# Second attention: the scores of a tile's four head groups issued together into four banks, and new orders

## The chip, the cores and the metric

One core of a Trainium2 chip runs the program in one launch. The metric is the device time in microseconds (us) on that core. The kernel before took 264.71 us, the median of three runs that lie between 264.69 and 265.05 us. TensorE is called PE here, as in the profile, VectorE DVE, ScalarE ACT and GpSimd POOL; PEld is PE's weight load.

## The reference

Two batches of 512 tokens with 128 channels pass a Flamingo-like block of two layers, all in float32:

```
layer 0: cross attention, 8 heads of 64 channels, keys = 512 tokens + 77 context rows, then out @ Wout
         gated add:  x1 = x + tanh(gx0) * attention(layernorm(x), layernorm(ctx))
         feed-forward with weights and activations rounded to few levels:
         512 hidden channels, a convolution of three taps along the tokens, silu;  x2 = x1 + tanh(gf0) * ...
layer 1: cross attention, 16 heads of 8 channels over the 77 context rows, rotary positions:
         scores = q @ k^T / sqrt(8);  p = softmax(scores);  out = p @ v;  y = out @ Wo^T + bo
         x3 = x2 + tanh(gx1) * y
         mixture of 8 experts (the best 2 by a router) plus a shared one, 64 hidden channels each
         out = x3 + tanh(gf1) * ...
```

The change is to the scores of the attention of layer 1, and to the order of everything.

## The kernel before

All data stay on the chip once loaded. The 512 tokens of a batch are four tiles of 128 rows. The work is cut into items, a kind with its numbers: for a batch b `x0` is the normalised input turned, `k`, `q`, `v` the projections of the first attention, `u` one head and tile of it (64 in all), `w` its product with the values, `o` its output projection, `n` the normalisation behind it, `f1` to `f4` the feed-forward (turning the input, first matrix with convolution by chunk, quantising by tile, second matrix by tile). For the second attention `a1` turns two tiles of the input, `a2` makes their queries, `a3` keys and values, `a4` is one tile with 8 of its 16 heads (16 items: 2 batches, 4 tiles, 2 halves), `a6` the product with the values and the output for two tiles. `m1` to `m4` are the experts.

An item has stages: F (front, on PE), B (back, on PE), A1 and A2 on ACT, D0 to D3 on DVE, P1 and P2 on POOL, and Ca or Cd, a copy by ACT or by DVE. For an `a4` item the chain is

- F: two matmuls at line 672, each with 32 rows of the array (four heads of 8 channels, kept apart by zeros in `KBD`), 308 columns, into two neighbouring banks of PSUM
- D1: the negated maximum of each head (`mx`, line 1152, DVE)
- A1: eight exponentials into `S` (line 910, ACT)
- B: five transposes back into the same two banks (line 518, PE)
- C: the copy of these into `PT` (line 787 on ACT or 789 on DVE); only then are the two banks free.

PSUM has eight banks. An item whose F says `F4` takes bank 4, and 5 as well if it is wide, as `a4`, `u`, `k`, `m2` and `m4` are; its F waits until what held these banks before is done with them (`banks_left`). For `a4` that is the copy C.

The order of the work is written out by hand in the table `PLAN`, one word a stage: each engine walks its own stages in the order of the table and waits for semaphores, and nothing overtakes. A word like `a4:B+20@2` puts 20 transposes of the identity into bank 2 ahead of the stage, which keep PE at work where it would wait. There are 85 such fillers. Semaphore `front_done` counts the F stages in PE's order, and DVE and ACT wait for an item's number in it (`NTH`).

## Time and profile before

| | us |
|---|---|
| median of the runs | 264.71 (264.69 to 265.05) |
| the profiled execution | 264.35 |
| its span, first to last instruction | 262.4 |
| PE busy | 254.0 (97%) |
| DVE busy | 217.1 (83%) |
| ACT busy | 192.2 (73%) |
| POOL busy | 31.1 (12%) |

Busy is the time in which an engine had an instruction under way. Matmuls are pipelined and their ends are modelled, so PE at 97% is not PE at its peak, and the fillers count as busy. Transfers matter only at the start: 0.52 MB is written and 4.99 MB read from memory in the whole span.

### The profile page before, as it was taken

Reading aid. Unit: us, or ns where it says so; the run is one execution under the profiler, and the core shown is the slowest. Engines: PE = TensorE matmul, PEld = TensorE weight load, DVE = VectorE, ACT = ScalarE, POOL = GpSimd, SP = SyncE. Lnnn points to the kernel's source line nnn. Section 1 sums busy time; section 2 is a strip of 40 time slices with the busy share of each in tenths; the row PEclk is TensorE's granted clock in tenths of the full one; section 3 lists DMA queues with packets and bytes.
Section 4 is the critical chain, followed back from the end, with each engine's and each line's share of the span. In section 5 each row is a group of like instructions: output and inputs, shape, how many; then the busy total and the mean of one; then the engine's idle time right before and its main releaser. Section 6 shows DMA issues by size and latency. Waiting matters only on the chain.

```text
span 262.4 us, 5607 instructions
## 1 busy us (share of the span) xinstructions
PE 254.0 (97%) x1869; PEld 189.2 (72%) x1869; DVE 217.1 (83%) x534; ACT 192.2 (73%) x463; POOL 31.1 (12%) x53
## 2 busy tenths in 40 slices
...
DMA packets 8848, 10.70 MB, mean 41 GB/s; under 512 B 1115, under 2 KB 5877, under 8 KB 8821
## 3 DMA queue, kind: packets, MB, share of 16 engines
...
q10 hardware_dynamic: 1029, 0.65, 0.8%
...
HBM read 4.99 MB, written 0.52 MB: 21 GB/s over the span
## 4 chain that ended last, share of the span: by engine, by line
PE 70%; DVE 18%; ACT 5%; issue 5%; POOL 1%; DVEq 0%; ACTq 0%; POOLq 0%
PE slot L518 19%; PE slot L608 13%; PE slot L589 6%; PE slot L590 6%; PE slot L564 3%; PE slot L615 3%; DVE mx L1152 3%; PE slot L570 2%; PE slot L761 2%; PE slot L755 2%; DVE RB L1157 2%; ACT S L910 2%; PE slot L706 2%; PE slot L749 2%; PE slot L579 2%
## 5 line engine op out<-in xcount | busy, mean ns | idle before, releaser
L1046 DVE TENSOR_REDUCE nm<-slot 128x1 f32<-128x589 f32 x64 | 47.6, 766 | 9.7 <-PE slot L590 9.3
L838 ACT ACTIVATE PR<-slot,nm 128x589 f32<-128x589 f32 x64 | 47.7, 749 | 9.3 <-DVE nm L1046 8.8
L518 PE MATMUL slot<-K,PR 128*128 128x128 f32 (+1 forms) x320 | 44.3, 276 | 0.2
L589 PE MATMUL slot<-KH,Q 128*128 128x296 f32 (+1 forms) x128 | 42.1, 345 | 0.2
L518 PEld LDWEIGHTS slot<-K,PR 128*128 128x128 f32 (+1 forms) x320 | 36.1, 142 | 8.1 <-ACT PR L838 5.0
L608 PE MATMUL slot<-PT,V 128*64 128x256 f32 (+1 forms) x320 | 38.1, 384 | 0.7 <-ACT PT L773 0.7
L773 ACT ACTIVATE PT<-slot 128x640 f32<-128x640 f32 x47 | 32.2, 705 | 8.3 <-PE slot L518 7.3
L590 PE MATMUL slot<-KL,Q 128*128 128x296 f32 (+1 forms) x128 | 36.1, 299 | 0.0
L910 ACT ACTIVATE S<-slot,mx 128x77 f32<-128x77 f32 x128 | 29.2, 365 | 6.3 <-DVE mx L1152 5.6
L608 PEld LDWEIGHTS slot<-PT,V 128*64 128x64 f32 (+1 forms) x320 | 22.1, 137 | 12.3 <-issue 3.5
L589 PEld LDWEIGHTS slot<-KH,Q 128*128 128x128 f32 x128 | 24.2, 189 | 3.6 <-issue 1.4
L590 PEld LDWEIGHTS slot<-KL,Q 128*128 128x128 f32 x128 | 24.3, 190 | 1.7 <-issue 1.4
L468 POOL TENSOR_TENSOR vex<-vex,mhalf 128x2 f32<-128x2 f32 (+1 forms) x15 | 10.8, 720 | 83.7 <-DVE vex L986 83.7
L484 POOL COPY REC<-rec 128x256 f32<-128x256 f32 x16 | 6.8, 422 | 111.4 <-DVE rec L1022 85.9
L775 DVE COPY PT<-slot 128x640 f32<-128x640 f32 x17 | 13.8, 815 | 1.8 <-PE slot L518 1.8
L1040 DVE TENSOR_TENSOR KL<-slot,KH 64x590 fp32r<-64x590 f32 x16 | 12.2, 765 | 2.7 <-ACT KH L871 2.3
L1152 DVE TENSOR_REDUCE mx<-slot 128x8 f32<-128x616 f32 x16 | 12.6, 794 | 0.3 <-PE slot L672 0.3
L838 ACT ACTIVATION_READ_ACCUMULATOR PR<-slot,nm 128x1 f32 x64 | 12.6, 197 | 0.0
L518 PE MATMUL slot<-K,S 128*128 128x128 f32 x80 | 11.7, 279 | 0.6 <-ACT S L910 0.6
L1033 DVE SCALAR_TENSOR_TENSOR Q<-slot,Q 64x512 fp32r<-64x512 f32 x16 | 11.0, 689 | 1.3 <-ACT Q L863 0.9
L871 ACT ACTIVATE KH<-slot 64x590 fp32r<-64x590 f32 x16 | 10.5, 654 | 2.3 <-PE slot L581 2.1
L518 PEld LDWEIGHTS slot<-K,S 128*128 128x128 f32 x80 | 8.8, 140 | 3.9 <-ACT S L910 3.5
...
## 6 DMA issues: line engine op xcount, KB each, us to landing
...
```

The costliest lines, as they stand in the source:

```text
L518: return pe.transpose(dst, src, ident[0:p, 0:p])
L589: pe.matmul(W[:, K0 + lo:K0 + hi], q, KH[:, g % 4, lo:hi], start=True, stop=False)
L590: mm = pe.matmul(W[:, K0 + lo:K0 + hi], q, KL[:, g % 4, lo:hi], start=False, stop=True)
L608: mm = pe.matmul(W[e * DH0:(e + 1) * DH0, 0:N], V[0:r, c, h * DH0:(h + 1) * DH0], PT[0:r, s, c, e, :], start=(c == 0), stop=(c == 4))
L773: engine.activation(dst, src, ACT.Copy).then_inc(pt_copied["ACT"], 1)
L775: engine.tensor_copy(dst, src).then_inc(pt_copied["DVE"], 1)
L838: act.activation(PR[:, s, :], W[:, K0:K0 + KEYS0], ACT.Exp, bias=nm0[:, s:s + 1], accum_out=sum0[:, b, p * 2 + f, t, e:e + 1]).then_inc(pr ...
L910: act.activation(S1[:, s, j * C:(j + 1) * C], W[:, at:at + C], ACT.Exp, bias=mx1[:, s, j:j + 1]).then_inc(exp1_ready, 1)
L1033: dve.scalar_tensor_tensor(out=Q[o, s, e, :], in0=W[r, 0:S], scalar=float(DH0) ** 0.5, in1=Q[r, s, e, :].bitcast(F32), op0=ALU.mult, op1=A ...
L1040: dve.tensor_tensor(KL[r, s, :], W[r, K0:K0 + KEVEN], KH[r, s, :].bitcast(F32), ALU.subtract).then_inc(k_ready, 1)
L1046: dve.tensor_reduce(nm0[:, s:s + 1], W[:, K0:K0 + KEYS0], AX.X, ALU.max, negate=True).then_inc(max_ready, 1)
L1152: dve.tensor_reduce(mx, w, AX.X, ALU.max, negate=True).then_inc(max1_ready, 1)
```

## The change

PE no longer has an F stage for the first half of a tile's `a4` pair. The F of the second half issues all four matmuls, on the four groups of 32 rows, into the four banks of both halves, and it waits for the former holders of all four. A new semaphore `scores1_ready` is counted up by the second and by the fourth matmul; DVE waits for it in place of `front_done`. D1, A1, B and C stay as they are, an item each. `PLAN` is written anew. The fillers are 68 now, where there were 85. Who makes the copies changes too:

| copies by DVE | before | after |
|---|---|---|
| `u` | 17 | 12 |
| `f3` | 4 | 6 |
| `a4` | 2 | 2 |

Up to the last `w` of batch 1 (its F on PE, its D1 on DVE) the two programs have the same items, and so behind it, but for copies: behind it DVE has lost one `QB` copy (line 814) and kept two `PT` copies.

```
-x0:F6 x0:A1 k:F0 q:F6 k:A1 k:F2 k:D1 q:A1 v:F4 q:D1 v:F0 k:A1 v:Ca k:D1 u:F6 u:F2 v:Ca u:F4 u:D1 u:D1 u:A1 u:A1 u:F0 u:D1
...
+x0:F2 x0:A1 k:F0 k:A1 k:D1 q:F6 k:F2 q:A1 q:D1 v:F4 v:F0 k:A1 k:D1 v:Ca v:Ca u:F6 u:F2 u:F4 u:D1 u:A1 u:F0 u:D1 u:B u:A1
...
-NTH = {x: n for n, x in enumerate(x for x, stage in ORDER["PE"] if stage == "F")}
+NTH = {x: n for n, x in enumerate(x for x, stage in ORDER["PE"] if stage == "F" and x[0] != "a4")}
...
+        scores1_ready = sem("scores1_ready")
...
                 if kind != "f1":
                     warm(item, "F")
+                if kind == "a4":
+                    if item[3] == 0:
+                        return
+                    for former in HAD[item[:3] + (0,)]:
+                        banks_left(former)
                 for former in HAD[item]:
                     banks_left(former)
...
                     _, b, t, h = item
                     pe.wait_ge(q1_ready, (b * QT + t) // TP + 1)
                     pe.wait_ge(kbd_ready, b + 1)
-                    for n in range(2):
-                        rows = slice((2 * h + n) * 32, (2 * h + n + 1) * 32)
-                        mm = pe.matmul(W[:, n * 512:n * 512 + G1 * C], Q1[rows, t * P:(t + 1) * P], KBD[rows, b],
+                    for g in range(G1):
+                        rows, scores = slice(g * 32, (g + 1) * 32), slot(("a4", b, t, g // 2))
+                        mm = pe.matmul(scores[:, g % 2 * 512:g % 2 * 512 + G1 * C], Q1[rows, t * P:(t + 1) * P], KBD[rows, b],
                                        start=True, stop=True)
+                        if g % 2:
+                            mm.then_inc(scores1_ready, 1)
+                    return
...
-                act.wait_ge(front_done, NTH[item] + 1)
+                if kind != "a4":
+                    act.wait_ge(front_done, NTH[item] + 1)
...
-                dve.wait_ge(front_done, NTH[item] + 1)
+                if kind == "a4":
+                    dve.wait_ge(scores1_ready, n)
+                else:
+                    dve.wait_ge(front_done, NTH[item] + 1)
...
                     if b == 1:
-                        dve.wait_ge(front_done, NTH["a4", 0, QT - 1, 1] + 1)
+                        dve.wait_ge(scores1_ready, 2 * QT)
```

The banks of the `a4` items of batch 1 are these, with what each must wait for. An item is written as tile and half.

| item | bank before, former holder | bank after, former holder |
|---|---|---|
| 0.0 | 2, `a4` of batch 0, tile 3 | 4, `a4` of batch 0, tile 3 |
| 0.1 | 0, `a2`, `a4` of batch 0 | 0, `a4` of batch 0 |
| 1.0 | 4, `a4` of batch 0, tile 3 | 4, item 0.0 |
| 1.1 | 2, item 0.0 | 2, `m1`, `a4` of batch 0 |
| 2.0 | 0, item 0.1 | 0, item 0.1 |
| 2.1 | 4, item 1.0 | 6, `a6`, `a2` |
| 3.0 | 6, `m1`, `a6` | 6, item 2.1 |
| 3.1 | 4, item 2.1 | 4, `m3`, item 1.0 |

What moves is seen on two engines in that same stretch. First ACT from the exponentials of tile 0 on: in these rows `S<-slot,mx` x8 is one A1 (x16 two in a row), `PT<-slot` a copy C, `LT<-slot` belongs to `a1` or `m1`, `SHT` and `lg` to `m3`, and `HM` and `slot<-slot` to `m2`. Before:

```order
L910 ACTIVATE S<-slot,mx 128x77 x16
L787 ACTIVATE PT<-slot 128x5x128
L910 ACTIVATE S<-slot,mx 128x77 x16
L787 ACTIVATE PT<-slot 128x5x128
L913 ACTIVATE LT<-slot 128x256
L910 ACTIVATE S<-slot,mx 128x77 x16
L918 ACTIVATE SHT<-slot 128x128
L923 ACTIVATE lg<-lg 128x16
L910 ACTIVATE S<-slot,mx 128x77 x8
L787 ACTIVATE PT<-slot 128x5x128 x2
```

After:

```order
L920 ACTIVATE S<-slot,mx 128x77 x8
L910 ACTIVATE LT<-slot 128x256
L923 ACTIVATE LT<-slot 128x256
L920 ACTIVATE S<-slot,mx 128x77 x8
L796 ACTIVATE PT<-slot 128x5x128
L920 ACTIVATE S<-slot,mx 128x77 x16
L796 ACTIVATE PT<-slot 128x5x128 x2
L920 ACTIVATE S<-slot,mx 128x77 x8
L928 ACTIVATE SHT<-slot 128x128
L933 ACTIVATE lg<-lg 128x16
L920 ACTIVATE S<-slot,mx 128x77 x8
L796 ACTIVATE PT<-slot 128x5x128 x2
```

Two rows `LT<-slot` stand now between the two A1 of tile 0, and the copies of a tile come behind both its A1 or, for tile 2, behind `SHT`, `lg` and the second A1. Before, a copy stood between most of the A1.

Then DVE, from the reciprocal of the second `a6` of batch 0 (`RB<-slot`) on: `mx<-slot` is D1 of an `a4` item, `RC` and `Q<-RC` are `a2`, `X<-slot,tg,X` with the three rows behind it is D2 of `a6`, `PT<-slot` a copy, `XN` D3 of `a6`, and `lg<-slot` starts `m3`. Before:

```order
L1157 RECIPROCAL RB<-slot 128x256
L1158 TENSOR_TENSOR A1T<-slot,RB 128x256
L1152 TENSOR_REDUCE mx<-slot 128x8
L789 COPY PT<-slot 128x5x128
L1238 SCALAR_TENSOR_TENSOR X<-slot,tg,X 128x256
L980 BN_STATS bnx<-X 128x6 x2
L981 BN_AGGR mvx<-bnx 128x2 x2
L986 TENSOR_SCALAR vex<-mvx 128x2
L1152 TENSOR_REDUCE mx<-slot 128x8
L789 COPY PT<-slot 128x5x128
L1152 TENSOR_REDUCE mx<-slot 128x8
L989 TENSOR_SCALAR XN<-X,mvx,vex 128x128 x2
L1163 COPY lg<-slot 128x16
```

After:

```order
L1170 RECIPROCAL RB<-slot 128x256
L1171 TENSOR_TENSOR A1T<-slot,RB 128x256
L1165 TENSOR_REDUCE mx<-slot 128x8 x2
L1155 SCALAR_TENSOR_TENSOR RC<-slot,COL,K 128x256 x2
L1158 TENSOR_TENSOR Q<-RC 128x256
L1251 SCALAR_TENSOR_TENSOR X<-slot,tg,X 128x256
L990 BN_STATS bnx<-X 128x6 x2
L991 BN_AGGR mvx<-bnx 128x2 x2
L996 TENSOR_SCALAR vex<-mvx 128x2
L1165 TENSOR_REDUCE mx<-slot 128x8 x2
L798 COPY PT<-slot 128x5x128
L1176 COPY lg<-slot 128x16
```

The two `mx` of a tile are neighbours now (`x2`). Before, single `mx` rows alternate with other work.

## Rows read from the trace of the kernel before

**Rows 1.** The page, section 1: busy time, share of span, instructions

```profile
PE 254.0 (97%) x1869; PEld 189.2 (72%) x1869; DVE 217.1 (83%) x534; ACT 192.2 (73%) x463; POOL 31.1 (12%) x53
```

**Rows 2.** Windows: PE, PEld, DVE, ACT, POOL busy (count), PEclk, DMA share, GB/s

```profile
0.00:165.90 165.90, 162.66 (x1165) 126.57 (x1166) 135.33 (x309) 126.29 (x256) 15.09 (x34) 1.00 0.22 60
165.90:204.40 38.50, 36.74 (x297) 26.31 (x295) 35.25 (x87) 30.73 (x93) 4.20 (x6) 1.00 0.01 2
204.40:224.50 20.10, 19.28 (x190) 12.45 (x187) 18.92 (x51) 16.87 (x66) 2.21 (x3) 1.00 0.01 2
224.50:241.90 17.40, 17.16 (x117) 10.45 (x115) 15.61 (x57) 9.33 (x27) 5.82 (x8) 1.00 0.02 6
241.90:262.40 20.50, 18.12 (x108) 13.41 (x108) 11.98 (x34) 9.03 (x22) 3.73 (x4) 1.00 0.08 23
```

**Rows 3.** Windows, line 672 alone: PE busy, PEld busy, PEclk; one item, then two

```profile
210.73:211.44 0.71, 0.71 (x4) 0.30 (x4) 1.00 0.00 0
203.04:203.90 0.86, 0.80 (x8) 0.31 (x8) 1.00 0.00 0
215.33:216.32 0.99, 0.96 (x8) 0.47 (x8) 1.00 0.00 0
```

**Rows 4.** Timeline of DVE, 208 to 224: start, us, what, [idle <-releaser]

```profile
208.01 0.87 DVE L1142 SCALAR_TENSOR_TENSOR RC<-slot,COL,K 128x256 f32<-128x256 f32 x2
...
209.25 0.59 DVE L989 TENSOR_SCALAR XN<-X,mvx,vex 128x128 f32<-128x128 f32 x2
209.77 1.75 DVE L1157 RECIPROCAL RB<-slot 128x256 f32<-128x256 f32 x1
...
211.89 0.79 DVE L1152 TENSOR_REDUCE mx<-slot 128x8 f32<-128x616 f32 x1
212.60 0.81 DVE L789 COPY PT<-slot 128x640 f32<-128x640 f32 x1
213.33 0.47 DVE L1238 SCALAR_TENSOR_TENSOR X<-slot,tg,X 128x256 f32<-128x256 f32 x1
...
214.72 0.80 DVE L1152 TENSOR_REDUCE mx<-slot 128x8 f32<-128x616 f32 x1
...
217.41 0.17 DVE L1163 COPY lg<-slot 128x16 f32<-128x16 f32 x1
...
221.16 1.76 DVE L1157 RECIPROCAL RB<-slot 128x256 f32<-128x256 f32 x1 [0.21 <-DVE cwt L1230]
...
223.68 0.80 DVE L1152 TENSOR_REDUCE mx<-slot 128x8 f32<-128x616 f32 x1 [0.30 <-PE slot L672]
```

**Rows 5.** Timeline of ACT, 200 to 219

```profile
200.19 1.83 ACT L910 ACTIVATE S<-slot,mx 128x77 f32<-128x77 f32 x8 [0.62 <-DVE mx L1152]
...
205.36 3.55 ACT L910 ACTIVATE S<-slot,mx 128x77 f32<-128x77 f32 x16 [1.51 <-DVE mx L1152]
209.96 0.70 ACT L787 ACTIVATE PT<-slot 128x640 f32<-128x640 f32 x1 [1.05 <-PE slot L518]
...
215.02 0.44 ACT L913 ACTIVATE LT<-slot 128x256 f32<-128x256 f32 x1
...
218.93 0.39 ACT L918 ACTIVATE SHT<-slot 128x128 f32<-128x128 f32 x1
```

**Rows 6.** Timeline of PE, 206 to 223

```profile
206.43 1.50 PE L684 MATMUL slot<-PT,V 128*32 128x256 f32 x24 [0.23 <-DVE X L1238]
...
222.85 0.79 PE L672 MATMUL slot<-KBD,Q 32*128 32x308 f32 x4
```

**Rows 7.** Timeline of DVE, 174 to 190

```profile
174.76 0.69 DVE L1091 TENSOR_TENSOR XL<-slot,XH 128x512 fp32r<-128x512 f32 x1 [0.40 <-PE slot L672]
...
189.85 0.43 DVE L814 TENSOR_SCALAR QB<-W 128x512 bf16<-128x512 f32 x1
```

**Rows 8.** Timeline of DVE near 238

```profile
238.57 1.03 DVE L1169 TENSOR_TENSOR lg<-lg,top 128x16 f32<-128x16 f32 x1
```

**Rows 9.** Timeline of POOL near 238

```profile
238.52 1.04 POOL L506 TENSOR_TENSOR HM<-HM,cwt 128x512 f32<-128x512 f32 x1
```

**Rows 10.** The page, section 4: the chain that ended last, by engine

```profile
PE 70%; DVE 18%; ACT 5%; issue 5%; POOL 1%; DVEq 0%; ACTq 0%; POOLq 0%
```

More of the change, by code:

```diff
@@ new lines @@
+u:D1 u:B u:D1 u:A1 u:Ca u:A1 s:D2 u:B u:Ca u:F6 u:Cd u:B u:F4 u:D1 u:F2 u:Ca u:A1 u:D1 v:F0 u:A1 u:D1 s:F1 u:B v:Ca
+u:B u:A1 u:Ca q:F0 u:Ca s:D1 q:A1 w:D0 u:B k:F6 u:F4 q:D1 k:A1 k:D1 w:P1 u:Ca w:F1 u:D1 w:A1 u:F6 w:D1 u:F2 u:D1 u:F0
+u:A1 u:B u:D1 u:A1 u:A1 u:D1 u:B u:Cd u:B u:A1 w:D0 u:Cd u:F4 w:P1 u:D1 u:B u:F6 u:Ca q:F3 u:D1 w:F2 u:A1 x0:D2 w:D0
+u:A1 u:B q:A1 u:Ca u:B q:D1 w:A1 u:F0 u:Ca w:D1 u:D1 w:P1 u:F4 u:Ca u:A1 u:D1 u:F2 u:A1 u:D1 u:A1 a3:F6 u:B u:B u:B
+a3:D1 u:Ca u:Ca u:F0 k:F4 g:F6 u:D1 u:Ca u:F2 u:D1 k:A1 w:F7 k:D1 u:A1 w:D0 x0:P2 u:A1 u:B g:D1 u:B u:Ca x0:D3 w:P1 u:F4
@@ new lines @@
+u:Ca u:D1 w:A1 u:A1 q:F6 w:D1 u:F0 q:A1 u:F2 u:B w:F7 u:D1 u:A1 u:Cd u:F4 w:A1 q:D1 w:D0 u:D1 u:A1 u:B w:D1 u:D1 u:Ca
+u:F6 u:B u:A1 u:D1 u:F0 u:A1 u:B u:Cd x0:F2 u:Ca u:D1 u:B u:A1 w:P1 a3:P1 a3:F4 x0:A1 u:Ca u:B k:F2 u:Ca a3:D1 k:A1 u:F6
+u:F0 w:D0 u:D1 k:D1 w:F5 u:A1 u:D1 u:B u:A1 q:F2 w:A1 u:B u:Ca w:D1 u:F4 w:P1 u:F6 u:D1 u:D1 q:A1 u:Cd q:D1 w:F3 u:A1
+u:A1 u:B u:B w:A1 u:Ca u:F0 u:Ca u:F4 w:D0 u:D1 w:D1 u:A1 u:D1 w:P1 w:F6 u:B u:F2 u:A1 w:A1 w:D1 u:D1 u:B u:Ca u:Cd
+o:F6 u:F0 o:D1 u:A1 u:B u:Ca u:D1 u:F6 u:A1 u:D1 w:D0 u:F4 q:F3 u:B u:D1 u:A1 u:Ca a3:P1 q:A1 w:P1 u:B q:D1 u:Cd w:F2
@@ new lines @@
+u:A1 u:B+2@0 u:F0 u:F6 u:Ca w:A1 o:F3 u:D1 u:F4 u:A1 u:D1 w:D1 u:B o:D1 n:P2 u:A1 o:F3 u:D1 o:D1 n:D3 u:B u:Ca u:A1 w:D0
+v:F0 k:F2 u:Ca u:B v:Ca u:F6 v:F0 k:A1 u:D1 u:Ca u:F4 k:D1 u:D1 u:A1 v:Ca u:A1 u:B u:Cd u:F2 k:F0 u:D1 u:A1 u:B o:F6
+k:A1 u:B u:Cd k:D1 u:Ca v:F7 o:D1 u:F4 w:P1 v:Ca u:D1 u:F2 u:F6 u:D1 u:A1 w:D0 u:A1 w:F1 u:D1 u:A1 u:B u:B n:P2 w:A1
+u:Ca n:D3 u:B u:Ca u:F4 f1:F0 u:D1 q:F2 u:Ca f1:A1 f1:D1 u:F6 u:A1 w:D1 u:D1 q:A1 w:D0 u:B f2:F3 q:D1 u:Ca u:F0 f2:A1 u:D1
+w:P1 u:F4 u:A1 w:F2 u:D1 u:A1 f2:D1 u:B u:B u:A1 u:B w:A1 u:Ca f2:A2 w:D1 u:Cd f2:F6 f2:D2 w:P1 u:F2 f2:F7 u:Ca u:F0 u:D1
@@ new lines @@
+k:F4 f2:A1 u:A1 f2:D1 u:D1 f2:A1 k:A1 u:B f2:D1 k:D1 w:D0 u:A1 w:F6 u:B f2:A2 f2:F7 w:P1 u:Ca w:A1 u:Ca f2:A1 u:F2 u:F4 f2:D2
+w:D1 u:D1 u:F0 f2:A2 u:D1 u:A1 w:F6 u:A1 u:B f2:D1 f2:A2 w:A1 u:D1 f2:D2 f2:D2 u:B f3:F7 u:A1 u:Ca u:B u:Ca u:F2 u:F4 u:Ca
+w:D1 f3:D1 f3:A1 u:D1 f3:F6 q:F0 u:D1 f3:D1 u:A1 f3:F1 f3:D1 u:B u:A1 w:D0 f3:A1 u:Ca f3:Cd u:B u:Ca f3:Cd u:F6 f3:A1 q:A1 u:D1
+w:P1 u:F2 f4:F5 w:F4 f4:A1 q:D1 f4:B u:D1 f4:D2 u:A1 u:B w:A1 u:F0 u:A1 u:Ca w:D1 f4:F5 u:D1 f4:A1 f3:F4 u:B f3:D1 f3:Cd w:D0
@@ new lines @@
+u:A1 u:F6 f4:B u:Ca f3:A1 u:B f4:D2 u:F2 u:Ca w:P1 u:F4 w:F1 f4:F0 u:D1 u:A1 f3:Cd u:D1 u:A1 u:D1 u:B u:A1 u:Ca w:D0 f4:A1
+u:B u:B u:Cd w:A1 u:F6 f4:B u:F2 w:P1 w:D1 u:Ca f4:P2 f4:D2 w:F4 f4:F5 u:D1 u:A1 u:D1 u:B u:A1 w:A1 w:D1 u:Ca u:F0 f4:A1
+f4:D3 u:D1 u:B u:F6 o:F4 u:D1 u:Ca u:A1 u:A1 o:F2 o:D1 u:B f4:B w:D0 u:B w:P1 o:D1 f4:D2 n:P2 u:Ca u:Ca f4:P2 a1:F1 n:D3
+w:F5 f4:D3 a1:A1 w:A1 a2:F2+3@0 a1:F7 w:D1 o:F6 a2:D1 a4:F2 o:F5 o:D1 o:D1 a4:F0 n:P2 a1:A1 a4:D1 a2:F4 a4:D1 a4:A1 a4:A1 a4:B+17@5 n:D3 f1:F5
```

47 lines of the change are left out of this document (12 added, 35 removed).

## The prediction

> **What bounds the kernel now.** I read the page's busy shares first, then the windows by stage, then the timelines of the stretch that the change touches. The page says PE at 97% and DVE at 83% [rows 1], and the chain of waits is PE for 70% and DVE for 18% [rows 10]. That invites the thought that work taken off PE shortens the run. The windows by stage say where that holds and where it does not [rows 2]. Up to 165.9 us, the end of the first attention, DVE is busy 135.33 of 165.9 us and PE 162.66: PE is the limit. From 241.9 on DVE is busy 11.98 of 20.5 us and PE holds the end. Between the two lies all of the second attention, and there DVE is the busier engine than its mean suggests: 35.25 of 38.5, 18.92 of 20.1 and 15.61 of 17.4 us. The counts of PE in these windows contain nearly all of the 85 fillers, which are no work. So the middle, 76 us long, is paced by DVE walking its list without a pause. A change there pays by what it does to DVE's list and to DVE's waits. PE's work there is cover.
>
> The waits of DVE in that middle are few: 0.40 us at the feed-forward of batch 1 [rows 7], 0.21 and 0.30 us later on [rows 4]. The three windows leave 3.25 + 1.18 + 1.79 = 6.2 us in which DVE was not busy, over 195 instructions [rows 2]; of this 2.9 us are waits of 0.1 us and over, the rest is the step from one instruction to the next.
>
> **The change part by part.** The profiled execution took 264.35 us with a span of 262.4; the median of the runs is 264.71. My sum is a difference against the profiled execution, and I add it to the median.
>
> *Scores four at a time.* One item's two matmuls occupy PE 0.71 us. Where two items of different halves happened to meet, the four took 0.86 us together in one place and 0.99 in another [rows 3], so the four groups of rows already overlap here. Eight tiles at 0.86 are 6.9 us, against 12 items alone at 0.71 and two such pairs (0.86 and 0.99), 10.4 us. PE loses 3.5 us of work, and 17 fillers with it. What hides both is DVE's list, so they cost and bring nothing: 0 us. If DVE's waits were all caused by PE they could bring at most the 2.9 us named above.
>
> *The copy.* DVE has one `QB` copy less in the middle: 0.43 us off [rows 7]. All other DVE work of the middle is the same set of instructions.
>
> *The collision.* A subtraction on 16 columns took DVE 1.03 us at 238.57, while POOL began a product on 512 columns at 238.52 [rows 8, 9]; a row of that size takes 0.17 [rows 4]. In another order it need not meet. Bounds: -0.9 and 0; I take -0.9.
>
> *First stage and tail.* Both have the same items on PE as before, and PE is their limit. The five `PT` copies that go from DVE to ACT there lie beside PE's work. I take 0 for both, with 0.7 us either way for other gaps; without cover each copy would be 0.7 us on ACT [rows 5].
>
> *The new waits, batch 1.* This is the main term. A tile now needs four banks at once, and its PE instruction waits for the last of the former holders. By the table of banks tile 1 needs bank 4 from item 0.0, tile 2 bank 0 from item 0.1, and tile 3 bank 6 from item 2.1; a bank comes back only when the copy C is done. ACT's list puts that copy behind both A1 of the tile (tile 0 with two `LT` between, tile 2 with `SHT` and `lg`). So I follow one tile's first `mx` to the next tile's first `mx`, once through ACT and once through DVE's own list. Prices: `mx` 0.71 to the next instruction and 0.80 to its end, a hand-over between engines 0.07 (a copy ends at 210.66, the scores that waited for its bank start at 210.73 [rows 3, 5]), a further A1 3.55 - 1.83 = 1.72, an `LT` 0.44, a copy 0.70 [rows 5], scores to `mx` 222.85 to 223.68 = 0.83 [rows 4, 6]. On DVE: `a2` 1.24, an `XN` pair 0.52, D1 of `a6` 2.12, copy 0.73, D2 of `a6` 1.39, `m3` 3.75 less the `mx` in it and the wait of 0.21, 2.83 [rows 4].
>
> Tile 0 to 1: 0.87 until A1 starts, 1.72, two `LT` 0.88, 1.72, copy 0.70, 0.07, 0.83 = 6.8 us. DVE has `mx`, `XN`, `mx`, `XN`, D1 of `a6` to do, 0.71 + 0.52 + 0.71 + 0.52 + 2.12 = 4.6. It waits 2.2 us.
> Tile 1 to 2: 0.87 + 1.72 + 1.72 + 0.70 + 0.07 + 0.83 = 5.9. DVE has two `mx`, `a2`, D2 of `a6`: 1.42 + 1.24 + 1.39 = 4.1. It waits 1.9.
> Tile 2 to 3: ACT first copies item 1.0, so A1 starts at about 1.3, ends at 3.0, then `SHT` and `lg` behind DVE's `lg`, to 3.5, A1 to 5.2, two copies to 6.6, and 0.9: 7.5. DVE has two `mx`, a copy, `XN` and `m3`: 1.42 + 0.73 + 0.52 + 2.83 = 5.5. It waits 2.0.
> Together 6.1 us. Behind tile 3 DVE's list is the old work with 0.9 us of waits, where before 1.3 us stood from 204.4 on. Net: +5.7. The other end is 0: were each bank back in time, as before, where the same chain found other DVE work beside it.
>
> *The new waits, batch 0.* The same walk there: tile 1's scores wait for the copy of item 0.0, which ACT has behind `XH` (DVE waits 0.65), the first chunk of the feed-forward stands behind them on PE (0.75), tile 2's scores wait for the quantising of tile 1 of the feed-forward (0.3), and behind these on PE stand the first `f4` and the 48 records of an `a6`, two times 1.4 us [rows 6], which DVE's first `f4` needs (1.15), then 0.45 more; the first `a2` wait is 0.46. That is 3.8 us, against 1.2 now (the 0.40 of [rows 7] among it), +2.6. The other end is 0. These hand-overs are less certain than those of batch 1, since each hangs on the one ahead of it, and all but one are of the size of waits that exist now; I take a third, +0.9.
>
> Sum: 0 - 0.4 - 0.9 + 0 + 5.7 + 0.9 = +5.3 us. The tail of 20.5 us starts when DVE frees bank 0 for the third `m4` of batch 0, at the end of that list, and PE cannot work ahead of its order, so it moves as a whole. Forecast 264.7 + 5.3 = 270.0 us.
>
> The rows show two items overlapping at 0.86 us [rows 3]. The Trainium skill, "TensorEngine Tiling (Array Packing)", section "Restrictions and Gotchas", says that row tiling raises PSUM pressure, since different row tiles write to different banks, and its section "PSUM Bottleneck" says that after such a speedup the copy out of PSUM may become the limit. This trace agrees in kind: the copy, 0.70 us, is what gives a bank back. That speaks against the change in the way of my main term. By its headline alone, up to four times faster for 32 rows, one would book the PE saving; I do not, because DVE paces this stretch.
>
> **Rivals.**
> *A, PE's relief reaches the end (faster).* The order feeds DVE as well as now or better, and scores come earlier for both halves. For it: overlap is real [rows 3], and 0.30 us of DVE's wait is for line 672 [rows 4]. Against it: the walk above uses durations that repeat all through the timeline. It would give -0.4 for the copy, down to -0.9 for the collision and some of the 2.9 us of waits: -2 us, 262.7, at best -4.2, 260.5.
> *B, the waits only change places.* The new waits are about as long as those removed, because PE or ACT run ahead further than I see: -0.4 to +0.4, 264.7.
> *C, the clock falls.* PE would wait up to 3.8 us at a time between tiles 1 and 2 (5.9 less some 1.9 of work), with no filler there. The granted clock is 1.00 in every window [rows 2], that is 2.4 GHz, with fillers in all long waits. Should it drop to 1.2 GHz, 5 us of PE work would take 10, so 275. Against it: nothing in this trace shows it drop after a wait.
> *D, the four matmuls do not overlap.* A tile would cost 1.42 us, and as the scores are on the walked chain, eight times 1.42 - 0.86 = 0.56 more, 4.5 us: 274.5. [Rows 3] speak against it twice.
>
> **How the numbers follow.** My forecast 0.66, its own range 267 to 272.5 (batch 1 at 4 to 6.1, batch 0 at 0 to 2.6, gaps 0.7). A 0.20, B 0.08, C 0.04, D 0.02. This kernel's runs tell no change from one of 0.2%, 0.5 us. Faster: A and a part of B, 0.22. Same: the middle of B, 0.06. Slower 0.72. The range that leaves out no more than 0.2 goes from 262.8, inside A, to 272.8.
>
> **What would show it.** In the profile after: line 678 in eight groups of 8 records, about 0.86 us from the first to the next instruction. On DVE, waits of 1.5 us and more ahead of the first `mx` of tiles 1, 2 and 3 of batch 1, released by line 678, and on PE waits ahead of line 678 released by the copy at line 796. DVE busy falls by some 4 us over the run, the span grows. The third `m4` of batch 0 starts about 5 us later than 241.95, and from there to the end it is 20.5 us. I am wrong if the largest waits of DVE there stay under 0.7 us, if A1 of the second half starts without waiting for its predecessors on ACT, or if the first stage ends more than 1 us away from 165.9.

## The result and the profile after

The changed kernel takes 274.38 us (median of four runs, 273.29 to 274.79), the kernel before 264.88 beside it (264.69 to 265.61). The ratio is 1.0336, with an interval of 1.0308 to 1.0364: 9.5 us slower. The direction was forecast; the forecast was 270.0 with a range up to 272.8, so the size was not. The profiled execution took 274.61 us with a span of 272.7, 10.3 more than the span before.

From the page of the kernel after, the busy times and the row of the granted clock in 40 slices:

```profile
PE 252.9 (93%) x1852; PEld 191.5 (70%) x1852; DVE 213.9 (78%) x531; ACT 194.6 (71%) x466; POOL 31.2 (11%) x53
PEclk9999999999999999999999999978998989999999
```

PE, DVE and POOL are busy for about as long as before or less [rows 1], DVE for 3.2 us less; ACT is busy for 2.4 us more, still 71% of its span. So for DVE, which paced the middle before, the 10.3 us are waits. The clock row is new: before it was full in every slice.

The windows of four stretches of the kernel after, where the granted clock (the number behind the bracket of POOL) stood at half, that is 1.2 GHz, and one behind them:

```profile
176.50:179.90 3.40, 3.40 (x16) 2.38 (x17) 1.59 (x3) 0.71 (x2) 0.00 (x0) 0.50 0.00 0
183.35:186.80 3.45, 3.02 (x14) 3.02 (x15) 3.38 (x6) 3.45 (x13) 0.00 (x0) 0.51 0.02 5
203.80:207.20 3.40, 3.40 (x14) 3.28 (x15) 2.71 (x5) 3.40 (x15) 1.39 (x2) 0.50 0.02 5
217.50:220.90 3.40, 3.40 (x13) 2.94 (x13) 2.74 (x5) 2.64 (x13) 0.00 (x0) 0.50 0.01 2
224.00:242.00 18.00, 15.93 (x157) 10.01 (x156) 14.30 (x51) 12.23 (x45) 3.56 (x5) 1.00 0.00 1
```

Where the time went is seen best on DVE, cut at the same instructions in both kernels: from the first score reduction (`mx`) of batch 0 to the first of batch 1, on to the last of batch 1, and on to the end. Windows of DVE alone, first of the kernel before (start and end, length, busy and count, clock, DMA share, GB/s):

```profile
170.25:204.49 34.24, 31.90 (x77) 1.00 0.01 1
204.49:223.68 19.19, 18.02 (x49) 1.00 0.01 2
223.68:262.40 38.72, 28.40 (x91) 1.00 0.05 15
```

and of the kernel after:

```profile
170.82:210.54 39.72, 32.02 (x79) 0.87 0.00 1
210.54:232.22 21.68, 14.86 (x43) 0.92 0.01 2
232.22:272.70 40.48, 30.15 (x95) 0.99 0.05 14
```

Length less busy is what DVE did not work (the two orders share the busy time out differently over the stretches, so only its sum is compared):

| | before | after | difference | forecast |
|---|---|---|---|---|
| up to the first stretch | 170.25 | 170.82 | +0.57 | 0 |
| batch 0, not busy | 2.34 | 7.70 | +5.36 | +0.9 |
| batch 1, not busy | 1.17 | 6.82 | +5.65 | +5.7 |
| behind it, not busy | 10.32 | 10.33 | 0.0 | 0 |
| busy in all three | 78.33 | 77.03 | -1.30 | -0.4 - 0.9 |
| sum | | | +10.3 | +5.3 |

One line is off by far, and it is off by 4.5 of the 5.0 us by which the sum is off. The other half microsecond is the later start, and it can't be put down to the change: the first reduction starts between 170.25 and 171.75 us in runs that are like the kernel before up to there, and between 170.26 and 171.38 in those that are like the kernel after.

Batch 1, the timeline of DVE in the kernel after (start, us, engine and line, what, and in brackets the idle time ahead of it and its releaser):

```profile
210.54 0.80 DVE L1165 TENSOR_REDUCE mx<-slot 128x8 f32<-128x616 f32 x1
211.76 0.79 DVE L1165 TENSOR_REDUCE mx<-slot 128x8 f32<-128x616 f32 x1
217.43 1.50 DVE L1165 TENSOR_REDUCE mx<-slot 128x8 f32<-128x616 f32 x2 [1.98 <-PE slot L678]
223.30 1.51 DVE L1165 TENSOR_REDUCE mx<-slot 128x8 f32<-128x616 f32 x2 [0.65 <-PE slot L678]
231.50 1.51 DVE L1165 TENSOR_REDUCE mx<-slot 128x8 f32<-128x616 f32 x2 [2.62 <-PE slot L678]
```

From tile to tile that is 6.9, 5.9 and 8.2 us, where the walk gave 6.8, 5.9 and 7.5. (Between tiles 2 and 3 ACT waits 0.76 us for the transposes ahead of its two copies, which stand on PE behind the matmuls of `a6`; the walk left them out.) In the kernel before, the first reductions of tiles 0, 1 and 3 were these (tile 2's is in [rows 4]):

```profile
204.49 1.50 DVE L1152 TENSOR_REDUCE mx<-slot 128x8 f32<-128x616 f32 x2
207.29 0.80 DVE L1152 TENSOR_REDUCE mx<-slot 128x8 f32<-128x616 f32 x1
...
218.38 0.79 DVE L1152 TENSOR_REDUCE mx<-slot 128x8 f32<-128x616 f32 x1
```

2.8 us from tile 0 to tile 1, 3.7 from tile 2 to tile 3. How the chain runs between tiles 0 and 1 is seen on ACT:

```profile
211.38 1.83 ACT L920 ACTIVATE S<-slot,mx 128x77 f32<-128x77 f32 x8 [1.79 <-DVE mx L1165]
213.57 0.39 ACT L910 ACTIVATE LT<-slot 128x256 f32<-128x256 f32 x1 [0.36 <-PE slot L519]
213.85 0.38 ACT L923 ACTIVATE LT<-slot 128x256 f32<-128x256 f32 x1
214.11 1.83 ACT L920 ACTIVATE S<-slot,mx 128x77 f32<-128x77 f32 x8
215.77 0.77 ACT L796 ACTIVATE PT<-slot 128x640 f32<-128x640 f32 x1
```

and on PE, whose four matmuls wait for the last of these:

```profile
216.59 0.80 PE L678 MATMUL slot<-KBD,Q 32*128 32x308 f32 x8 [2.30 <-ACT PT L796]
```

The copy ends at 216.54, the scores start at 216.59, DVE's reduction at 217.43: each step as priced. A tile's four matmuls occupy PE 0.73 us to the next instruction, where the prediction took 0.86 from [rows 3].

Batch 0, DVE's waits of 0.4 us and more in the kernel after:

```profile
177.76 1.51 DVE L1165 TENSOR_REDUCE mx<-slot 128x8 f32<-128x616 f32 x2 [1.17 <-PE slot L678]
180.78 0.75 DVE L1110 SCALAR_TENSOR_TENSOR YC<-slot,cw,YC 128x511 f32<-128x511 f32 x1 [1.51 <-ACT YC L892]
189.71 0.69 DVE L1118 TENSOR_REDUCE aq<-slot 128x1 f32<-128x512 f32 x1 [0.42 <-PE slot L519]
194.01 0.80 DVE L1165 TENSOR_REDUCE mx<-slot 128x8 f32<-128x616 f32 x1 [0.51 <-DVE aq L1121]
197.83 0.35 DVE L1215 SCALAR_TENSOR_TENSOR X<-slot,aq,X 128x128 f32<-128x128 f32 x1 [1.12 <-PE slot L740]
207.89 0.48 DVE L1155 SCALAR_TENSOR_TENSOR RC<-slot,COL,K 128x256 f32<-128x256 f32 x1 [1.29 <-PE slot L670]
```

The walk had 0.65 and 0.75 for the first two and 1.15 for the fifth; the last, for the queries of `a2`, it had at under half a microsecond. The three that exceed it lie in or right behind the stretches at half clock. The tail moved as a whole: the third `m4` of batch 0 starts at

```profile
252.24 0.77 PE L519 MATMUL slot<-K,HM 128*128 128x128 f32 x5
```

and 20.5 us are left from there, as before.

### The profile page after: what moved, and what is told of

Its sections match the earlier page's. It is cut to its first block, busy times and chain, and to the rows that moved or that the text cites. A ratio compares the mean times of both kernels' runs of the same rounds, so it can differ in the third digit from the quotient of the medians.

```text
span 272.7 us, 5563 instructions
## 1 busy us (share of the span) xinstructions
PE 252.9 (93%) x1852; PEld 191.5 (70%) x1852; DVE 213.9 (78%) x531; ACT 194.6 (71%) x466; POOL 31.2 (11%) x53
## 4 chain that ended last, share of the span: by engine, by line
PE 73%; ACT 11%; DVE 10%; issue 5%; ACTq 0%; DVEq 0%
PE slot L519 23%; PE slot L614 12%; PE slot L595 5%; PE slot L596 5%; ACT S L920 5%; PE slot L570 3%; PE slot L770 2%; PE slot L764 2%; PE slot L678 2%; PE slot L621 2%; PE slot L576 2%; PE slot L715 2%; PE slot L758 2%; PE slot L585 2%; PE slot L670 1%
## 5 line engine op out<-in xcount | busy, mean ns | idle before, releaser
L595 PE MATMUL slot<-KH,Q 128*128 128x296 f32 (+1 forms) x128 | 41.5, 341 | 0.2
L782 ACT ACTIVATE PT<-slot 128x640 f32<-128x640 f32 x52 | 35.5, 704 | 7.8 <-PE slot L519 7.1
L519 PE MATMUL slot<-K,S 128*128 128x128 f32 x80 | 14.0, 323 | 3.4 <-ACT S L920 3.4
L519 PEld LDWEIGHTS slot<-K,S 128*128 128x128 f32 x80 | 11.2, 167 | 7.4 <-ACT S L920 5.8
L796 ACT ACTIVATE PT<-slot 128x640 f32<-128x640 f32 x14 | 10.0, 732 | 6.2 <-PE slot L519 6.1
L678 PE MATMUL slot<-KBD,Q 32*128 32x308 f32 x64 | 6.9, 505 | 7.8 <-ACT PT L796 6.6
```

The costliest lines, as they stand in the source:

```text
L519: return pe.transpose(dst, src, ident[0:p, 0:p])
L595: pe.matmul(W[:, K0 + lo:K0 + hi], q, KH[:, g % 4, lo:hi], start=True, stop=False)
L678: mm = pe.matmul(scores[:, g % 2 * 512:g % 2 * 512 + G1 * C], Q1[rows, t * P:(t + 1) * P], KBD[rows, b], start=True, stop=True)
L782: engine.activation(dst, src, ACT.Copy).then_inc(pt_copied["ACT"], 1)
```

## The experiments

Times are medians, with the kernel before beside them on the same chip; that one moved between 265.1 and 265.9 from one chip to the next, so the ratios are what is compared. Each edit is made on the kernel after or the kernel before, as said.

The first stage moves by one or two microseconds from run to run, so differences of that size are read from the profiled executions by stretch, in us: the start of the first score reduction of batch 0, from there to the first of batch 1, on to the last of batch 1, and on to the end.

| kernel | first reduction | batch 0 | batch 1 | behind it |
|---|---|---|---|---|
| before | 170.25 | 34.24 | 19.19 | 38.7 |
| before, no fillers (e4) | 170.03 | 35.84 | 19.19 | 38.7 |
| before, two tiles packed (e16) | 170.73 | 34.04 | 19.14 | 38.7 |
| before, three tiles packed (e5) | 170.82 | 34.07 | 20.59 | 38.7 |
| before, four tiles packed (e6) | 172.01 | 34.08 | 26.92 | 38.7 |
| before, more on DVE (e7) | 171.75 | 34.26 | 23.70 | 38.8 |
| before, copy moved (e9) | 170.46 | 34.25 | 19.24 | 38.7 |
| before, two copies moved (e12) | 170.31 | 34.26 | 21.03 | 38.7 |
| old then new (e10) | 170.82 | 36.55 | 27.62 | 40.5 |
| new then old (e11) | 170.51 | 41.34 | 18.37 | 38.7 |
| the same with fillers (e14) | 170.47 | 38.92 | 19.97 | 38.7 |
| after | 170.82 | 39.72 | 21.68 | 40.5 |
| after with fillers (e1) | 171.38 | 37.58 | 21.75 | 40.5 |
| after, scores two at a time (e2) | 172.92 | 38.95 | 21.90 | 40.6 |
| after, copies first (e3) | 170.29 | 38.51 | 20.55 | 40.5 |
| after, fillers and copies first (e13) | 170.26 | 37.59 | 21.00 | 40.5 |

### The kernel after with fillers at PE's waits (e1)

```
-a4:F2 a4:F6 a2:D1
+a4:F2 a4:F6+13@7 a2:D1
...
-f2:F0 f2:D2
+f2:F0+12@0 f2:D2
...
-a4:F4 a4:F2 a4:D1
+a4:F4 a4:F2+20@3 a4:D1
```

Nine stages have fillers ahead of them like these, 107 in all (the expectation counts 109).

> The kernel after, with 109 more fillers (transposes of the identity) written at PE's longest waits of the second attention, in banks that are free there; all else as after. In the kernel after the granted clock stood at half in four stretches of 3.41 us, and it was lower at no place of the kernel before. Theory (half of the loss is the clock): the fillers keep the clock up, the four stretches go or shrink to one, and of the 9.5 us that the change cost 2.5 to 3 come back: about 271.5 us. Rival (PE is cover there, so a slow PE is cover too): the clock goes up but the time stays within 0.5 us of 274.4. Third way: fillers that run longer than the wait push PE's own work back, and the time is above 274.4.

272.84 us against 265.14, ratio 1.028 (1.0235 to 1.0325), granted clock 1.00 throughout. Half of the expected gain came: some 1.5 us. The windows of DVE over the same first two stretches:

```profile
171.38:208.96 37.58, 32.12 (x79) 1.00 0.00 1
208.96:230.71 21.75, 14.69 (x41) 1.00 0.01 3
```

Not busy in batch 0: 5.46 us, where the kernel after has 7.70; in batch 1: 7.06, where it has 6.82. So the lower clock costs 2.2 us in batch 0 and nothing in batch 1, where the tiles follow each other by 7.0, 5.9 and 8.2 us, as in the kernel after. The waits that shrank are those that came out above the walk:

```profile
177.86 1.51 DVE L1165 TENSOR_REDUCE mx<-slot 128x8 f32<-128x616 f32 x2 [0.73 <-PE slot L678]
180.04 0.75 DVE L1110 SCALAR_TENSOR_TENSOR YC<-slot,cw,YC 128x511 f32<-128x511 f32 x1 [0.67 <-ACT YC L892]
197.11 0.35 DVE L1215 SCALAR_TENSOR_TENSOR X<-slot,aq,X 128x128 f32<-128x128 f32 x1 [1.13 <-PE slot L740]
```

0.73, 0.67 and 1.13 against the walk's 0.65, 0.75 and 1.15; the 1.29 ahead of `a2` is gone, with 0.30 now ahead of the first reduction of batch 1. In batch 1 the chain runs through ACT, and PE at half pace fits in beside it.

### The new order with the old code (e2)

```
-                    for g in range(G1):
-                        rows, scores = slice(g * 32, (g + 1) * 32), slot(("a4", b, t, g // 2))
+                    for n in range(2):
+                        rows = slice((2 * h + n) * 32, (2 * h + n + 1) * 32)
```

and no wait for the other half's banks, on the plan of the kernel after.

> The order of the kernel after (its plan, its banks, its copies) with the code of the kernel before: each item issues its own two score matmuls and waits for its own two banks only. It tells the pack from the new order. Theory (the pack's demand for four banks at once makes the waits): the scores of the first half no longer wait for the second half's banks, the waits of 2 to 2.6 us before the first score reduction of tiles 1 to 3 of batch 1 shrink to about 1 and the time is 268 to 270 us. Rival (the order alone makes them, since the first half's bank is the late one: tile 1 needs the bank of item 0.0 for its own first half): the time stays within 1 us of 274.4.

275.84 us against 265.14, ratio 1.040 (1.0355 to 1.0445). The theory fell and the rival was right: without the pack the new order is no faster. That it came out 1.5 us slower (the kernel after has 1.0336, up to 1.0364; the intervals just touch) is not read as a gain of the pack: its first reduction starts 2.1 us later, and from there to the end it takes 101.4 us, where the kernel after takes 101.9. Why it starts late is open. The wait ahead of tile 1 stays:

```profile
218.87 1.50 DVE L1152 TENSOR_REDUCE mx<-slot 128x8 f32<-128x616 f32 x2 [1.99 <-PE slot L672]
```

The table of banks says why: in the new order item 1.0 takes bank 4 from item 0.0, so even its own two matmuls wait for that copy.

### ACT's copies of tile 0 first (e3)

```
-m1:A1 a6:D1 a4:A1 a4:Ca a4:F4
+m1:A1 a6:D1 a4:Ca a4:A1 a4:F4
...
-a4:B a4:A1 a4:A1 a2:D1 a4:Ca
+a4:B a4:Ca a4:A1 a2:D1 a4:A1
```

> The kernel after with ACT's order changed at tile 0 of batch 1 alone: the copy of item 0.0 stands ahead of the second group of eight exponentials, and the copy of item 0.1 right behind its own exponentials. Theory (the bank comes back too late, because the copy stands behind both groups of exponentials): tile 1 gets its banks 1.7 us earlier and tile 2 some of it too; the first score reduction of tile 1 no longer waits 2 us but under 1, and the time falls by 1 to 3 us, to 271.5 to 273.5. Rival (DVE and ACT are late at the next tile anyway, the wait moves on to it): no change, 274.4 within 0.5.

272.03 us against 265.14, ratio 1.0254 (1.0199 to 1.031): 2.4 us below the kernel after by the medians, with intervals that just touch. On DVE the first reductions of tiles 1, 2 and 3 of batch 1 read:

```profile
214.25 1.50 DVE L1165 TENSOR_REDUCE mx<-slot 128x8 f32<-128x616 f32 x2 [0.48 <-ACT S L920]
218.32 0.80 DVE L1165 TENSOR_REDUCE mx<-slot 128x8 f32<-128x616 f32 x1
228.64 1.51 DVE L1165 TENSOR_REDUCE mx<-slot 128x8 f32<-128x616 f32 x2 [2.85 <-PE slot L678]
```

From tile 0 (208.80) to tile 1 it is now 5.5 us for 6.9, and to tile 2 4.1 for 5.9. The place of a copy in ACT's list is what sets when the four banks are together: that part of the theory holds. But to tile 3 it is 10.3 us for 8.2, so that of 3.2 us won 2.1 are handed back, as the rival had it, and batch 1 is 1.1 us shorter. The rest of the gain, 1.2 us in batch 0 and 0.5 ahead of it, lies where the edit changes nothing; in batch 0 the clock stood at half for 6.8 us, where it did so for 10.2 in the kernel after.

### The kernel before without fillers (e4)

```
-f1:F6+18@5 f1:A1 a4:F4
+f1:F6 f1:A1 a4:F4
...
-f2:D1 a4:B+20@2
+f2:D1 a4:B
```

and so for all 85.

> The kernel before with all 85 fillers left out, and nothing else changed. Theory (the chip's granted clock falls behind PE's waits of over a microsecond, and the fillers are what held it at 1.00): stretches at half clock appear, in the middle and perhaps at the start, and the time is 267 to 270 us. Rival (the fillers only look busy, and the clock stays up with matmuls nearby): granted clock 1.00 throughout and the time within 0.5 us of 264.9. In both cases DVE's list in the middle is untouched, so that all of a loss is the clock.

265.66 us against 265.14, ratio 1.0032 (1.0003 to 1.0061). The clock fell as the theory said, to a mean of 0.72 of full over 175 to 185 us and 0.77 over 185 to 195, which is half clock for some 10 us:

```profile
175.00:185.00 10.00, 7.07 (x29) 5.34 (x31) 8.95 (x15) 9.30 (x27) 0.01 (x1) 0.72 0.00 1
```

but it cost 0.5 us by the medians, not 2 to 5. The profiled execution puts it at 1.6 us, all in batch 0, where as long a time at half clock costs the kernel after 2.2 us. So in both orders most of a slow PE is covered: 10 us at half pace hold back up to 5 us of PE's work, by an estimate from the clock rows alone.

### Old order, pack on two or three tiles (e16, e5)

On the kernel before with the changed code, the four-at-a-time path is taken for the tiles of a set:

```
+PACKED = ((0, 0), (1, 0), (1, 2))
...
-                if kind == "a4":
+                if kind == "a4" and item[1:3] in PACKED:
                     if item[3] == 0:
                         return
...
-                    for g in range(G1):
+                    for g in range(G1) if (b, t) in PACKED else range(2 * item[3], 2 * item[3] + 2):
```

and for the second run `PACKED = ((0, 0), (1, 0))`.

> The order, banks and copies of the kernel before, word for word, with the four-at-a-time scores on three of the eight tiles: those where the two score stages already stand next to each other on PE or nearly (batch 0 tile 0, batch 1 tiles 0 and 2). It is the pack alone. The run of the new order with the old two-at-a-time code took 275.8 us against 274.4 with the pack, so the order carries the whole loss. Theory (the pack as such is harmless or helps a little, DVE's list paces): 264.9 within 0.6 us. Rival (asking for four banks at once costs here too): tile 2's first half waits for item 1.0's copy and the time is 266 or more.

> The order of the kernel before with the four-at-a-time scores on two tiles alone, batch 0 tile 0 and batch 1 tile 0, whose four banks are free at that time and whose two score stages stand next to each other on PE. With tile 2 of batch 1 packed as well it took 266.5 us, and DVE waited 1.33 us ahead of that tile. Theory (the pack as such neither costs nor brings anything; what costs is that the first half waits for what the second half stood behind): 265.2 to 265.9 where the kernel before takes 265.6, no wait at 216.5. Rival (the packed instruction group or its semaphore costs by itself): 266.2 or more, with the loss spread over both tiles.

Three tiles: 266.53 us against 265.88, ratio 1.0046 (1.0025 to 1.0068). Two tiles: 264.76 against 265.31, ratio 0.9988 (0.9964 to 1.0012). Where both halves stand together on PE and their banks are free, the pack costs nothing and brings nothing that can be measured; tile 2 of batch 1 costs 1.3 us of DVE's time. In the run with three tiles:

```profile
216.54 0.80 DVE L1166 TENSOR_REDUCE mx<-slot 128x8 f32<-128x616 f32 x1 [1.32 <-PE slot L679]
```

and PE ahead of it:

```profile
215.01 0.77 PE L520 MATMUL slot<-K,S 128*128 128x128 f32 x5 [1.10 <-ACT S L921]
215.71 1.30 PE L679 MATMUL slot<-KBD,Q 32*128 32x308 f32 x12
```

and ACT's copy of item 1.0, which gives back bank 4, the one that the second half needs:

```profile
214.80 0.76 ACT L797 ACTIVATE PT<-slot 128x640 f32<-128x640 f32 x1
```

The packed scores stand where the second half stood, behind the transposes of item 1.1, and these wait for its exponentials. PE's own order is what they waited for last, which neither theory nor rival had. But the copy ends at 215.56 and the scores start at 215.71, so the bank would have held the first half back almost as long, as the rival said; this run does not tell the two apart.

### Old order, tile 1 packed too (e6)

```
+PACKED = ((0, 0), (1, 0), (1, 1), (1, 2))
...
-a4:A1 a4:D1 a4:B a2:D1
+a4:A1 a2:D1 a4:B a4:D1
```

> As the run with three packed tiles, and tile 1 of batch 1 packed too: its four matmuls stand where its second half stood, behind the copy of item 0.0, and DVE's score reduction of item 1.0 is placed behind the first step of the second a2, which PE needs first. Theory (the four-bank wait costs where tiles follow each other closely): DVE waits about 1.5 us ahead of that reduction, ACT behind it, and the time is 1 to 2 us above the run with three tiles, about 266.5. Rival (the work beside it hides it): within 0.5 us of that run.

272.80 us against 265.88, ratio 1.0257 (1.021 to 1.0304). 6 us above the run with three tiles, where 1 to 2 were expected: the wait is there, the size is not. DVE:

```profile
213.19 0.80 DVE L1166 TENSOR_REDUCE mx<-slot 128x8 f32<-128x616 f32 x1 [2.86 <-PE slot L679]
221.95 0.80 DVE L1166 TENSOR_REDUCE mx<-slot 128x8 f32<-128x616 f32 x1 [2.49 <-PE slot L679]
```

In the kernel before item 1.0 was reduced at 207.29, 2.8 us behind item 0.0, while items 0.0 and 0.1 were still being exponentiated, since its own banks had been free for long. Packed, it waits for item 0.0's copy, and 213.19 is 7.1 us behind item 0.0 (206.09 in this run). The 2.86 us are at full clock. The wait recurs at tile 2, where the granted clock is at half in addition, as it is for 10 us from 218.4 us on. So the demand for four banks makes waits of the size that the new order has in batch 1, in an order that had none; but the 6 us are those of a packed tile, a reduction moved in DVE's list and a lower clock together, and no run takes them apart.

### One batch in each order (e10, e11)

The plan of one kernel up to the first scores of batch 1, the rest from the other; the pack only where the order is the new one.

> The order of the kernel before up to the first scores of batch 1 (scores two at a time), and from there the order of the kernel after with its pack on all four tiles of batch 1. By the milestones of the two traces the part up to there cost 5.2 us (0.8 of it a later rise of the clock at the start) and the tiles of batch 1 cost 6.8, with 1.7 back behind them. Theory (the two parts add up): 264.9 + 6.8 - 1.7 = 270.0 us, 269 to 271. Rival (the losses overlap, each is given back where the other is not there): 267 or less, or 272 and more where the batch-1 order rests on what the batch-0 order leaves done.

> The other half: the order of the kernel after, with its pack, up to the first scores of batch 1, and from there the order of the kernel before with scores two at a time. It measures the term that the prediction took at a third, +0.9 us, of a walk that gave 2.6. Theory (batch 0 cost what the milestones say, with the clock): 264.9 + 5.2 = 270.1 us, 269 to 271, or some less where the start's clock rises as early as before. Rival (the walk's full size is right and the rest was the clock only): 267.5. Second rival (the third was right): 265.8.

Old then new: 277.31 us against 265.88, ratio 1.0443 (1.0396 to 1.049). It says little. At the seam a wait arose that neither kernel has, since `a6` of batch 0 on PE now waits 3.70 us for an `LT` copy that ACT makes later, and then starts at half clock:

```profile
214.84 1.76 DVE L1171 RECIPROCAL RB<-slot 128x256 f32<-128x256 f32 x1 [5.45 <-PE slot L699]
```

Without those 5.45 us it would be near 272; that is arithmetic, not a measurement, and the run is left as inconclusive.

New then old: 271.00 against 265.88, ratio 1.0204 (1.0136 to 1.0273), 5.1 us, as expected. That is over five times the 0.9 us that the order of batch 0 was given in the forecast, though not for batch 0 alone: at this seam DVE waits 1.15 us ahead of the first reduction of batch 1, where the kernel after does not wait, and batch 1 behind it is 0.8 us shorter than in the kernel before.

### New order in batch 0 with fillers (e14)

```
-a4:F2 a4:F6 a2:D1
+a4:F2 a4:F6+13@7 a2:D1
...
-a1:P1 a4:B f2:D1
+a1:P1 a4:B+12@4 f2:D1
```

and at three more stages, on the run "new then old" (e11).

> The run with the new order for batch 0 and the old one for batch 1 (271.0 us, granted clock 0.986), with 57 more fillers at five of PE's waits in batch 0 and nothing else changed. It splits the batch-0 loss of 5 to 6 us into the clock's part and the waits' own. Theory (the walk's full size, +2.6, was right and the clock made the rest): the clock is 1.00 and the time falls by about 2, to 268.5 to 269.3 where the kernel before takes 265.6. Rival (the waits alone make it): it stays at 270.5 to 271.5 though the clock is at 1.00.

269.47 us against 265.31, ratio 1.0159 (1.0122 to 1.0196): 4.2 us above the kernel before, where it was 5.1. Between theory and rival. In the batch-0 stretch itself 2.4 us came back (38.92 us long for 41.34), but the clock, full up to 205 us, fell once behind it:

```profile
205.00:215.00 10.00, 8.34 (x77) 5.00 (x77) 7.13 (x20) 5.94 (x21) 1.43 (x2) 0.83 0.01 2
```

and batch 1 took 19.97 us for 18.37, with the same program there but the clock at a mean of 0.91 for 1.00. So of two falls the fillers removed one and moved the other into batch 1, where it cost 1.6 us.

### More work on DVE in the kernel before (e7)

```
                     dve.tensor_reduce(mx, w, AX.X, ALU.max, negate=True).then_inc(max1_ready, 1)
+                    if b == 1:
+                        dve.tensor_reduce(mxx[:, n - 9:n - 8], K[:, K_CQ:K_CQ + 616], AX.X, ALU.max)
```

> The kernel before with one more reduction on DVE (over 616 constants in SBUF, its result unused) behind each of the eight score reductions of batch 1. It asks whether DVE's list sets the pace of the kernel before from 204 to 242 us, which the prediction rested on. A score reduction takes 0.71 us to the next instruction, so eight are 5.7 us, or less if the source in SBUF is read faster. Theory (DVE paces): what DVE's added work lasts, less at most 1.5 us of waits that it fills, comes out at the end: 269 to 270.5. Rival (the chain from ACT's bank copy to the scores paces, as in the kernel after): under 267.5.

269.13 us against 265.63, ratio 1.015 (1.0114 to 1.0185). One of the eight:

```profile
206.71 0.78 DVE L1155 TENSOR_REDUCE mxx<-K 128x1 f32<-128x616 f32 x1
```

Eight take 5.7 us of DVE's list at 0.71 to the next instruction. 4.0 us came out by the ratio, and the stretch of batch 1 grew by 4.5. DVE's list does set the pace, with a good microsecond of slack: the premise of the prediction.

### Fewer copies on DVE in the kernel before (e9, e12)

```
-a4:B a4:Cd a4:A1 a6:B
+a4:B a4:A1 a4:Ca a6:B
```

and, for the second, also

```
-m3:A1 a4:A1 a4:B a4:B a4:B a4:Ca m2:F0
+m3:A1 a4:Ca a4:A1 a4:B a4:B a4:B m2:F0
```

> The kernel before with one copy fewer on DVE: item 0.1 of batch 1 is copied by ACT, between the eight exponentials of item 1.0 and those of item 1.1, where ACT waits 0.38 us. Nothing else changes. Theory (DVE paces this stretch): 0.73 us less on DVE, 0.3 us later on ACT for item 1.1, which DVE's list covers: 264.4 to 264.7 where the kernel before takes 265.1. Rival (ACT's list is just as tight there, 9.66 of 10.5 us busy, and the copy of tile 2 gives the bank back later): 0 to +0.4.

> As the run before it, and ACT copies item 2.0 of batch 1 ahead of the exponentials of item 3.0, where it stood behind them: the first shared expert's matmul gets its bank 1.7 us earlier and the scores of item 3.1 with it. Theory (the copy's place in ACT's list sets when banks come back, as the run with the copies first showed on the kernel after, -2.4 us): DVE's wait of 0.30 us ahead of the last score reduction goes, 0.2 to 0.5 us below the run with the moved copy alone. Rival: that reduction is late for other reasons (PE's own list), no change, or +0.3 since the exponentials of item 3.0 come 0.7 us later.

The first: 265.64 us against 265.63, ratio 1.001 (0.9989 to 1.0031). DVE's list lost 0.73 us of work and got it back as waits, 0.48 us of it for transposes that ACT's exponentials released later:

```profile
215.78 0.82 DVE L789 COPY PT<-slot 128x640 f32<-128x640 f32 x1 [0.48 <-PE slot L518]
```

So work added to DVE shows and work taken from it does not: ACT is just as tight here. The second: 269.76 against 265.63, ratio 1.0186 (1.0138 to 1.0234), though its runs lie far apart, from 266.26 to 272.37 with granted clocks of 0.999 down to 0.987, and why is open, so only the trace is used; its batch 1 is 1.8 us longer than that of the first. PE has the transposes of item 3.0 ahead of the scores of item 3.1, and those waited for the exponentials that the copy had pushed back:

```profile
223.21 0.77 PE L518 MATMUL slot<-K,S 128*128 128x128 f32 x5 [1.98 <-ACT S L910]
```

An earlier copy helped a little in the kernel after and hurt here. The rule "copies first" does not carry over; the chain does.

### Both mends on the kernel after (e13)

The fillers of the first run and the copies of the third.

> The kernel after with both mends: the fillers at PE's waits (which took the time to 272.8 with the clock at 1.00 throughout) and ACT's two copies of tile 0 ahead (which took it to 272.0). Theory (clock and bank wait are separate losses): they add up, 274.4 - 1.5 - 2.4 = 270.5 us, within 0.7. Rival (the fillers helped where the copy made PE wait, so one takes the place of the other): 271.7 to 272.3.

271.33 us against 265.63, ratio 1.0242 (1.0203 to 1.0281), clock 1.00. By the medians 0.8 above the sum and below the rival; by the ratios it lies hardly below the copies alone (1.0254). The intervals do not separate the two, but the trace shows the rival's mechanism. Batch 0 is as long as with the fillers alone; in batch 1 the copies bring 0.75 us in place of 1.1, since 20 fillers now stand in a wait that the earlier copy has made shorter:

```profile
211.51 2.35 PE L519 MATMUL slot<-K 128*128 128x128 f32 x20
213.78 0.80 PE L678 MATMUL slot<-KBD,Q 32*128 32x308 f32 x8
```

The scores of tile 1 start 5.9 us behind the first reduction of batch 1, where with the copies alone they start 4.6 us behind it. No version of either kernel came out below the kernel before; the two-tile pack and the moved copy equal it.

## Why the prediction was wrong in size and right in kind

**The step that failed is the term "the new waits, batch 0".** The walk gave 3.8 us of waits against 1.2, +2.6, and of this "a third, +0.9" was taken, because each hand-over hangs on the one ahead of it. Measured is +5.36. With the clock held at full it is 5.46 - 2.34 = +3.1 (e1), so the walk was about right at its full size, with three of its waits within 0.1 us; the discount had no row behind it. That a chain's links depend on one another makes its waits less certain, but it does not make them shorter. The other 2.2 us are the granted clock, for which the sum had no term. With 2.6 in place of 0.9, and 2.2 for the clock, the sum would have given 273.9, where 274.38 was measured. The order of batch 0 in front of the old batch 1 costs 5.1 us (e11). No run mended the waits of batch 0 themselves; that they are not the pack's is shown by the run without it, where that stretch is 38.95 us long, against 38.51 with the pack and as long a time at half clock (e2, e3).

**The clock was kept as a rival instead of a bound.** Rival C, "the clock falls", had a chance of 0.04 and a price of 5 us, placed between tiles 1 and 2 of batch 1. It fell four times, three of them in batch 0, and cost 2.2 us there and nothing in batch 1 (e1), where it did fall at 217.5 us, between tiles 1 and 2. The four runs of the kernel after go with it: 273.29 us at a mean clock of 0.994, 274.14 to 274.79 at 0.987 to 0.974. What PE did before the first fall: it waited 1.28 us ahead of tile 1's scores and 0.28 before that, with two groups of transposes, some 1.6 us, between. "Nothing in this trace shows it drop after a wait" was true, but the trace before held 85 fillers in just those waits, so it could not have shown it; the kernel before without them drops too (e4). The Trainium skill, "TensorE: Matmul & The Clock Gate", section "Part 1: The HAM clock gate", says that the clock has two levels and follows how busy PE has been; this trace agrees, with 0.50 and 1.00.

**The new waits of batch 1: right in size, wrong in cause.** +5.7 forecast, +5.65 measured, and the intervals of 6.8, 5.9 and 7.5 us came out at 6.9, 5.9 and 8.2. But the pack is not what makes them in this order. The same waits stand with scores two at a time (e2), since the order itself gives item 1.0 the bank of item 0.0. The pack makes such waits where the order has free banks for the first half (e6). Two routes to one chain: a bank comes back only by a copy that ACT has behind both groups of exponentials. Moving that copy made tiles 1 and 2 come 3.2 us earlier and batch 1 as a whole 1.1 us shorter (e3). The Trainium skill, "TensorEngine Tiling (Array Packing)", section "PSUM Bottleneck", says that the copy out of PSUM may become the limit once the matmuls are faster; here the copy is in the chain with the pack and without it (e2), by its place in ACT's list and not by its 0.70 us.

**The copy and the collision: right.** DVE's busy time fell by 1.30 us, as 0.4 + 0.9, and the four subtractions of `lg` on 16 columns take 0.174 to 0.177 us each in the kernel after.

**First stage and tail: right within the 0.7 us allowed.** The start came 0.57 us later, which is within what programs that are alike up to there differ by; the tail did not change.

**PE's work is cover, DVE paces: right, with a limit.** Two tiles packed in the old order brought nothing that can be measured (e16, 0.9988), and work added to DVE came out at 4.0 of 5.7 us (e7). But taking work from DVE brought nothing either (e9): ACT stands right behind it, so the bound looks to be the loop DVE, ACT, PE and back, not one engine. That is also why rival A, at 0.20, did not come: a relieved PE reached nothing (e16).
